# A layer-norm, attention and quantized-FFN kernel: statistics of the second half made ahead, block loads requested a step ahead, reloads in four parts

## What is computed

```python
xn = _layernorm(x, axis=-1)                       # x: 4 x 1024 x 1024, f32
s = _L0_attn_ref(xn)                              # softmax over the 4 batch rows, per position l
g = _silu(_L0_ffn_ref(xn, gate_codes, gate_scales, up_codes, up_scales, down_codes, down_scales))
x = x + s * g
# _L0_ffn_ref: NF4 codes (blocks of 64) are turned into Wg, Wu (2752 x 1024) and Wd (1024 x 2752), then
gate = jnp.einsum('bsh,ih->bsi', x, Wg)
up = jnp.einsum('bsh,ih->bsi', x, Wu)
inter = jax.nn.silu(gate) * up
return jnp.einsum('bsi,hi->bsh', inter, Wd)
```

## Time and profile before

| what | us |
|---|---|
| median of 3 runs | 2674.68 (2670.05 to 2675.88) |
| profiled execution | 2672.88, of it 2671.1 between first and last instruction |
| PE busy | 2445.3 (92%) |
| DVE busy | 1650.6 (62%) |
| ACT busy | 1010.7 (38%) |
| first product of step 5 to first product of step 45 | 242.58 to 1091.28 |

### The profile page before, as it was taken

The page is one execution under the profiler, slowest core; times in us unless marked ns, Lnnn a source line. Parts: engine busy times, 40 slices in busy tenths (PEclk is TensorE's granted clock), DMA queues, the critical chain, the costliest instruction groups (busy, mean ns, idle before and its releaser), DMA issues.

```text
span 2671.1 us, 30439 instructions
## 1 busy us (share of the span) xinstructions
PE 2445.3 (92%) x11214; PEld 1114.0 (42%) x11214; DVE 1650.6 (62%) x2721; ACT 1010.7 (38%) x1303; POOL 457.0 (17%) x318
## 2 busy tenths in 40 slices
PE   2459999898888897999999999999999999999999
PEld 1224444443333343444444444444444444444444
DVE  6767877876687774678788788655451341341341
ACT  5467666566666652444545542111001000000000
POOL 3441111112222211111111011112011011011011
PEclk9679999999999998999999999999999999999999
DMA  6354555655656547665655564324886776776864
GB/s 220 105 165 155 183 174 189 193 174 181 221 178 210 172 147 294 234 216 192 202 195 207 197 203 172 135 91 166 319 334 247 326 286 255 323 280 260 325 273 158
DMA packets 176016, 571.14 MB, mean 214 GB/s; under 512 B 23968, under 2 KB 49232, under 8 KB 158076
## 3 DMA queue, kind: packets, MB, share of 16 engines
q1 hardware_dynamic: 140876, 280.82, 30.7%
q10 hardware_dynamic: 34992, 288.37, 28.6%
HBM read 380.38 MB, written 188.75 MB: 213 GB/s over the span
## 4 chain that ended last, share of the span: by engine, by line
PE 66%; DVE 12%; issue 7%; DMA 6%; POOL 5%; ACT 3%; SPq 1%; DVEq 0%; POOLq 0%; ACTq 0%
PE ps L1554 37%; PE ps L1683 29%; DVE arena L1220 3%; DMA arena<-xnsc 3%; DMA isc<-arena 1%; POOL arena L707 1%; DVE arena L1164 1%; ACT arena L756 1%; DVE arena L1189 1%; DMA arena<-in_gu 1%; POOL arena L678 1%; DVE arena L1214 1%; POOL arena L704 1%; DVE st L1104 1%; ACT arena L890 1%
## 5 line engine op out<-in xcount | busy, mean ns | idle before, releaser
L1554 PE MATMUL ps<-arena 128*128 128x512 f16 x7200 | 1600.5, 385 | 118.6 <-ACT arena L931 45.3
L1554 PEld LDWEIGHTS ps<-arena 128*128 128x128 f16 x7200 | 710.5, 99 | 996.3 <-issue 62.5
L1683 PE MATMUL ps<-arena 128*128 128x512 f16 x3696 | 797.9, 379 | 0.0
L756 ACT ACTIVATE arena<-arena,bias_t 128x1024 f32<-128x1024 f32 (+1 forms) x520 | 574.3, 1141 | 41.9 <-DMA arena<-in_gu 27.9
L1683 PEld LDWEIGHTS ps<-arena 128*128 128x128 f16 x3696 | 361.6, 98 | 436.1
L1220 DVE TENSOR_TENSOR arena<-arena 128x512 f16<-128x512 f32 x364 | 310.8, 864 | 63.4 <-ACT arena L890 62.2
L697 POOL TENSOR_TENSOR arena<-arena 128x512 f32<-128x512 f32 x52 | 77.2, 1484 | 1066.3 <-DVE arena L1347 894.4
L1214 DVE CAST arena<-arena 128x512 f16<-128x512 f32 x308 | 172.0, 570 | 132.5 <-POOL arena L707 59.5
L721 POOL TENSOR_TENSOR arena<-arena 128x512 f32<-128x512 f32 x64 | 82.2, 1292 | 686.6 <-DMA arena<-in_xt 385.3
L931 ACT ACTIVATE arena<-ps,gate_back 128x512 f32<-128x512 f32 x84 | 57.4, 683 | 364.8 <-PE ps L1554 364.6
L1072 ACT ACTIVATE arena<-arena,e_d 128x512 f32<-128x512 f32 x48 | 34.6, 721 | 424.3 <-DVE arena L1483 219.4
(11 more groups left out here) (109 smaller groups left out, 1329.8 us busy)
## 6 DMA issues: line engine op xcount, KB each, us to landing
isc<-arena SPq DMA_DIRECT2D x308, 256.0 KB, 2.0
arena<-wdsc ACTq DMA_DIRECT2D x28, 2816.0 KB, 10.0
arena<-isc ACTq DMA_DIRECT2D x28, 2816.0 KB, 18.2
arena<-xnsc SPq DMA_DIRECT2D x48, 1024.0 KB, 10.7
wsc<-arena ACTq DMA_DIRECT2D x21, 1792.0 KB, 6.6
arena<-in_gu ACTq DMA_DIRECT2D x43, 512.0 KB, 4.1
wdsc<-arena SPq DMA_DIRECT2D x77, 256.0 KB, 2.1
arena<-in_x SPq DMA_DIRECT2D x32, 512.0 KB, 5.9
```

What stands on the lines that cost most here:

```text
L756: a_.activation(buf, src, ACT.Prelu, bias=bias_t[:, i:i + 1], scale=scale, alpha=alpha).then_inc(ramps, 1)
L1554: ins = t_.matmul(ps[:, bank, :], wreg[:, b, w, wa, k, :], xreg[:, j, o, k, xa, :], start=start and (k, wa, xa) == (0, 0, 0), stop=stop an ...
L1683: ins = t_.matmul(ps[:, bank, :], ring_w[b][:, k, wa, g, :], ring_i[b][:, k, xa, :], start=first and (k, wa, xa) == (0, 0, 0), stop=r not ...
```

## The change

Five edits.

1. The statistics of tiles 16 to 31 are no longer made in pairs beside their normalisation. The tiles are loaded once more and their statistics taken in steps 4 (six tiles, one in each slot), 6 and 7 (five each, slots 0 to 4). SP loads tile tt+2 when the statistics of tile tt are done, since there are two slots. All 16 are aggregated and all roots taken in slot 1 of step 8. Tiles are normalised from step 8 on, a pair every second step (`NORM_AT` 8 to 22), the first in slot 4, the second in slot 5.
2. The x jobs move from steps 22 to 35 to steps 26, 27, 30, 31, 34, 35, 38, 39. Their blocks are requested one step earlier on SP.
3. The x jobs of even steps (26, 30, 34, 38) have their casts on VectorE and their items in slots 0 to 2 (`SOON_CUT`); those of odd steps (`X_ACT`) keep the casts on ScalarE.
4. `reloads` takes a part, 0 to 3; the transfers of steps 41 to 45 are dealt out to the start of ScalarE's step, after its first ramps, after `sil_a`, and after its second ramps.
5. In step 44 the items of the down weights move from slot 1 to slot 5, and after a LAST step the two memsets come behind the product that TensorE waits for.

```diff
-NORM_AT = {6 + 2 * i: (16 + 2 * i, 17 + 2 * i) for i in range(8)}
-XJOB_AT = {s: (2 + i // 4, i % 4) for i, s in enumerate([s for s in SPARE if s >= 22][:8])}
+STAT_AT = {4: range(16, 22), 6: range(22, 27), 7: range(27, 32)}
+ROOTS_AT = 8
+NORM_AT = {8 + 2 * i: (16 + 2 * i, 17 + 2 * i) for i in range(8)}
+XJOB_AT = {s: (2 + i // 4, i % 4) for i, s in enumerate([s for s in SPARE if s >= 24][-8:])}
+X_ACT = [XJOB_AT[s] for s in XJOB_AT if PASS[s][1]]
...
+SOON_CUT = [0, 6, 10, 14, 14, 14, 14]
...
-                if tt == 16:
+                if tt >= 16:
+                    sp.wait_ge(stat, 32)
+                    if nat_use(tt):
+                        sp.wait_ge(xs_out[nat_slot(tt)], 16 * nat_use(tt))
...
+            def load_stat(tt):
+                h, n, q = tokens(tt)
+                if tt < 18:
                     sp.wait_ge(e_lo, 5 * 7)
+                else:
+                    sp.wait_ge(stat, 2 * (tt - 18) + 2)
+                sp.dma_start(nat[nat_slot(tt)], x[n, h * CH + q * P:h * CH + (q + 1) * P, :]).then_inc(nat_in[nat_slot(tt)], 16)
...
-                if s in XJOB_AT:
-                    load_blocks(("x",) + XJOB_AT[s])
+                if s + 1 in XJOB_AT and s not in XJOB_AT:
+                    load_blocks(("x",) + XJOB_AT[s + 1])
...
+                if s + 1 in XJOB_AT and s in XJOB_AT:
+                    load_blocks(("x",) + XJOB_AT[s + 1])
...
+                if s == 3:
+                    load_stat(16)
+                    load_stat(17)
+                for tt in STAT_AT.get(s, ()):
+                    if tt + 2 < 32:
+                        load_stat(tt + 2)
...
-                    if s == 41:
-                        act.wait_ge(prod, prod_at(40, "p5"))
-                        load_xb(0, 5)
-                        load_xb(0, 6)
-                        act.wait_ge(prod, prod_at(39, "p3"))
-                        load_w(0, 4, 7)
-                        load_w(0, 2, 4)
-                    elif s == 42:
-                        act.wait_ge(prod, prod_at(41, "r"))
-                        act.wait_ge(prod, prod_at(40, "p3"))
-                        for o in (0, 4, 2, 3):
-                            load_xb(0, o)
+                if (s, part) == (41, 0):
+                    act.wait_ge(prod, prod_at(40, "p5"))
+                    load_xb(0, 5)
+                elif (s, part) == (41, 1):
+                    load_xb(0, 6)
+                elif (s, part) == (41, 2):
+                    act.wait_ge(prod, prod_at(39, "p3"))
+                    load_w(0, 4, 7)
+                elif (s, part) == (41, 3):
+                    load_w(0, 2, 4)
+                elif (s, part) == (42, 0):
+                    act.wait_ge(prod, prod_at(41, "r"))
+                    act.wait_ge(prod, prod_at(40, "p3"))
+                    load_xb(0, 0)
...
+            def stats(tt):
+                dve.wait_ge(nat_in[nat_slot(tt)], 16 * nat_use(tt) + 16)
+                for k in (0, 1):
+                    v_.bn_stats(st2[:, tt - 16, 6 * k:6 * k + 6], nat[nat_slot(tt)][:, 512 * k:512 * k + 512]).then_inc(stat, 1)
...
-                if s in DOWN_AT and slot == (5 if jobs else 1):
+                if s in DOWN_AT and slot == (5 if jobs or s == NSTEP else 1):
                     d_items(*DOWN_AT[s])
...
-                if s in NORM_AT and slot == 3:
-                    lnorm(NORM_AT[s], 2)
+                for tt in list(STAT_AT.get(s, ()))[slot:slot + 1]:
+                    stats(tt)
+                if s == ROOTS_AT and slot == 1:
+                    all_roots()
+                if s in NORM_AT and slot >= 4:
+                    normal(NORM_AT[s][slot - 4])
```

More of the change, by code:

```diff
@@ L106 @@
 JOB = {c: i for i, c in enumerate(JOBS)}
-INNER = {c: i for i, c in enumerate(c for c in JOBS if c[0] == "i")}
+CAST_HERE = {c: i for i, c in enumerate(c for c in JOBS if c[0] == "i" or c[1:] not in X_ACT)}
 NEARLY = 8
@@ L851, in reloads @@
                     load_w_second(1)
-                    for o in (0, 4, 2, 3):
-                        load_xb(1, o)
-                elif s == NSTEP + 1:
+                    load_xb(1, 0)
+                elif (s, part) == (NSTEP, 1):
+                    load_xb(1, 4)
+                elif (s, part) == (NSTEP, 2):
+                    load_xb(1, 2)
+                elif (s, part) == (NSTEP, 3):
+                    load_xb(1, 3)
+                elif (s, part) == (NSTEP + 1, 0):
                     act.wait_ge(prod, prod_at(43, "p2"))
                     load_w(0, 1, 2)
+                elif (s, part) == (NSTEP + 1, 1):
                     load_xb(1, 1)
+                elif part or h == 0:
+                    return
                 elif s == NSTEP + 3:
@@ L1107, in lnorm, with roots @@
                     step(v_.bn_aggr(mv[:, i, :], st[:, i, :]), i == m - 1)
-                va, r, t = y[:, 0, 0:m], y[:, 1, 0:m], y[:, 2, 0:m]
-                step(v_.tensor_scalar(va, mv[:, 0:m, 1], EPS, 2.0 ** (-2 * XS), ALU.add, ALU.mult))
+                roots(mv[:, 0:m, 1], y[:, 0, 0:m], y[:, 1, 0:m], y[:, 2, 0:m], True)
+                dve.wait_ge(ln_out, tiles[0] // 8 + 1)
+                for i, tt in enumerate(tiles[:mine]):
+                    v_.tensor_scalar(nat[nat_slot(tt)], nat[nat_slot(tt)], mv[:, i, 0:1], y[:, 1, i:i + 1],
+                                     ALU.subtract, ALU.mult).then_inc(xn_done, 1)
+            def roots(var, va, r, t, shared):
+                step(v_.tensor_scalar(va, var, EPS, 2.0 ** (-2 * XS), ALU.add, ALU.mult))
                 step(v_.tensor_scalar(r.bitcast(I32), va.bitcast(I32), -0.5, float(0x5F375A86), ALU.mult, ALU.add))
@@ L1315, in background @@
                 for c in jobs:
-                    for i in range(JOB_CUT[slot], JOB_CUT[slot + 1]):
+                    at = SOON_CUT if c[0] == "x" and c[1:] not in X_ACT else JOB_CUT
+                    for i in range(at[slot], at[slot + 1]):
                         c_item(c, i)
```

87 lines of the change are left out of this document (56 added, 31 removed).

## The result

| | us |
|---|---|
| before, median of 4 runs | 2673.91 (2670.05 to 2675.88) |
| after, median of 4 runs | 2653.93 (2650.41 to 2658.59) |
| ratio | 0.9928, 95% interval 0.9907 to 0.9949 |
| predicted | 2617, range 2599 to 2636 |
| profiled execution | 2672.88 before, 2658.59 after; between first and last instruction 2671.1 and 2656.8 |

The kernel is 0.7% faster, some 20 us, where 57 were forecast. The sign was right, and the size lies outside the range. Ratios leave out one execution that was far slower at a lower granted clock (2712.66 us, experiment 8); the median and the span given there still count it.

A forecast was written before the change was run, and what follows sets the result against it. TensorE, busy 92%, was taken as the bound, losing 119.4 us to waits and slow clock. After: 18 + 10.3 + 31 + 5.3 = 64.6, so 54.8 won from 2672.9: 2618, stated as 2617 us, range 2599 to 2636.

The forecast's parts named there:

- The sum: Steps 5 to 45: TensorE's losses fall from 119.4 to 64.6 us, so 54.8 us are won.
- The 10.3 us of silA I leave: Steps 11, 15, 19, 23: waits for silA stay at 10.3 us, as loads keep their order beside the same steps.
- Statistics: Steps 4 to 8: statistics made ahead stand at loads and delay c21; 18 us lost, 10 more than before.
- p7(7), forecast at 2.3 us: Step 6's statistics make c21(5) late: a wait of 2.3 us, and 1.3 for the clock.
- Steps 13, 17, 21: Normalisation and c21 waits go once statistics leave steps 12, 16 and 20: 21.4 us won.
- x cycles: Four cycles from step 24, VectorE the bound, block landing 8.5 us: 31 us lost against 59.8 before.
- the wait of 7.29 us the largest: Steps 24 to 37: the wait in front of the cycle from 650.21 was called the largest, 7.29 us.
- The turn: Reloads dealt out and down-weight items moved to slot 5: 5.3 us lost against 20.0 before.
- I keep 2 us of the 12.85, bounds 0 and 8: Step 42: of TensorE's 12.85 us wait for c21(40) at p7(42), 2 us remain, between 0 and 8.
- bound by bytes, not by their order: Rival, chance 0.08: at the turn the 12.85 us come back nearly whole, 2628 us.
- only about 1 MB at a time now stands before a store: Turn: the same bytes are moved, but with only about 1 MB at a time before a store; part of the 5.3 us term.
- Casts beside GpSimd's sums: Even x jobs on VectorE: first two casts could take 1.84 us beside a sum; each step could cost a sum's length more.

The follow-up runs named there:

- experiment 8: Changed kernel with the turn's reloads of x in order of first use and spread over one step more: 2657.63 us, ratio 0.9947.
- experiment 2: Changed kernel with four ramps, not five, ahead of sil_a in even steps 4 to 38: 2640.83 us, ratio 0.9882.
- experiment 4: Changed kernel with the first pair of x blocks of each cycle requested behind the stage stores, not ahead: 2641.68 us, ratio 0.9886.
- experiment 6: Changed kernel with only a quarter of each x-operand load at the turn (256 KB in place of 1 MB): 2641.47 us in one run.
- experiment 1: Changed kernel with edit 1 undone, statistics back beside the normalisation in steps 6 to 20: 2654.07 us, ratio 0.9933.
- experiment 5: Changed kernel with the high parts of all eight x blocks cast on ScalarE, as before: 2651.19 us, ratio 0.9927.
- experiment 7: Kernel before with edits 4 and 5 alone: 2668.25 us beside 2669.78, ratio 0.9996.

## Why the prediction was wrong in size

**The sum.** 54.8 us were to be won from step 5 to step 45. By the same count 16.7 were (119.4 less 102.7), and the profiled execution is 14.3 us shorter. Of the 38 us between, 14 are at sil_a, 17 in steps 24 to 39 and 11 at the turn as far as step 45, less 2 that the statistics cost less than forecast. That is 2 us too many, since the places are waits and slow clock, while the total charges each step 18.29 us. That is from a step's first start to its last end; from start to start a step without a wait takes 18.13 us (experiment 2: 38.01 us for two with four half tiles). So the work is 723 us and not 729.7, and 125 us were lost before and 109 after; the difference stays. Three terms failed, by 11 to 17 us each in this execution. For each there is a run that takes its cause away and is 12 to 13 us faster than the changed kernel by the medians (experiments 2, 4 and 6, the last a single execution).

**"The 10.3 us of silA I leave": a step that failed (24 measured, 16 to 24 in five executions).** It argued that SP's and the code loads' order beside those steps stays the same. It does. But how long TensorE waits depends on its own position too: each pause of TensorE, 5 us in every fourth step, was also a head start for ScalarE and VectorE. With it gone, the ramps of steps 14 and 18 start at 9.4 to 10.3 us into TensorE's step in place of 6.7 to 8.4, and sil_a is as much later, with the slow clock on top. Experiments 1 and 2 show the coupling: undoing edit 1 brings sil_a's waits from step 5 to 24 down from 18.3 to 7.4 us, and moving one ramp takes those of steps 11 to 23 away. The term should have been worked out like the others: when does ScalarE reach its fifth ramp, if TensorE no longer waits?

**Statistics (18 forecast, 16 measured).** The size was near, and the mechanism right in the main: VectorE stands at loads of x, and TensorE for c21 at p7(5) and longest in step 9 (6.24 us, forecast 7.0, though at the normalised tile and not at c21). Two errors in it cancel. VectorE's waits for the tiles were 0.6 to 3.2 us each, not a whole landing, since its other work covered part of each round, and at p7(7), forecast at 2.3 us, TensorE didn't wait. But it waited 3.84 us at p7(6), with 2.7 of slow clock, which was put at nothing: the sixth tile of step 4 stands behind c21(3), VectorE waits 3.19 us for it, and so is late with c21(4).

**Steps 13, 17, 21 (0 forecast, 0 measured).** Right. Yet the gain of 21.4 us was not the kernel's: with the edit undone the median is the same (experiment 1), and step 24 starts at 637.1 us, in the midst of the 633.5 to 643.5 of the changed kernel's executions.

**x cycles (31 forecast, 48 measured): a cost put at nothing.** The blocks' landing was near (8.5 to 10.3 us for 8.5). The casts moved to VectorE bought nothing (experiment 5): a block cast there trades a wait for sil_a for one for c21. (The prediction also called the wait of 7.29 us the largest; the one at 739.40 has 7.65.) The step that failed is this: two loads of 512 KB requested ahead of seven stage stores on the same queue were taken as free for the stores. They cost VectorE 17.1 us of stage slots, and the kernel 12 us (experiment 4).

**The turn (5.3 forecast, 17.6 measured).** "I keep 2 us of the 12.85, bounds 0 and 8": 6.91 was left, within the bounds. Put at nothing were the slow clock behind it (2.9), the weight block's wait (3.1) and a c21 just behind step 45 (1.5). The order of the requests counted, for VectorE's slot waits fell from 20.0 to 11.4 us. But the rival "bound by bytes, not by their order", given 0.08, holds for the rest: requests dealt out leave 18 us of loss (experiment 7), and with a quarter of the bytes 5.7 are left (6). The step that failed is "only about 1 MB at a time now stands before a store". The loads of 1 MB were requested 6.0 and 11.5 us apart and took 10.9 us to land (median), with a weight store and weight loads between them, so that from 1000.3 to 1030.0 some transfer of ScalarE's queue was always under way. The Trainium skill (DMA: Bandwidth & Descriptors, "Queues, rings and completion order") says that each DMA engine changes between the queues that have work, packet by packet. The landing of 10.0 us for a store beside the loads and 5.4 beside quarter loads agrees with it: a store shares for as long as any load is under way. By that, the rival deserved a larger chance. And the load of weight block (0,0,1) in step 43 was overlooked: it now stands behind a load of 1 MB on its queue, 3.1 us.

**Casts beside GpSimd's sums.** The prediction weighed that an instruction on VectorE is slower while GpSimd makes a sum. In the x jobs moved to VectorE it didn't happen, since GpSimd's first sums are over by then: the first two casts at 779.38 took 0.75 us, against 1.84 in an inner job. It reached another place: a low part of a weight block at 770.72 took 1.76 us, while GpSimd's first sum of x ran, against 0.69 us for the one at 764.32. About 1 us a place; it decides nothing here.

## What to carry to other kernels

A wait on the engine that bounds is also slack for the others: before counting it as won, work out when each of them would be late if that engine came on at once. A term left "as it is" needs the same arithmetic as one that changes. And a load requested early is not free for the stores queued or under way beside it: what counts is bytes in the stretch and who holds a buffer until they have landed.

## What the runs showed of the hardware

- A store of 256 KB took 10.0 us to land beside loads of 1 MB on another queue and 5.4 beside loads of 256 KB (median of those issued from 1000 to 1024 us), and 2.0 us at 993.8, with nothing beside it. The mean DMA share over 985 to 1030 us was 0.77 and hid where the stores were held. In pieces of 5 us (the share is the last number but one) it is 0.49 ahead of the loads and 1.04 beside them:

```profile
995.00:1000.00 5.00, 5.00 (x24) 2.24 (x23) 3.54 (x7) 2.38 (x3) 1.28 (x1) 1.00 0.49 185
1010.00:1015.00 5.00, 5.00 (x25) 2.29 (x24) 1.63 (x3) 1.84 (x3) 0.80 (x1) 1.00 1.04 397
```

- Waits of 3.06 to 5.14 us in every fourth step brought 7.3 us of slow clock with them (24 products in 6.8 to 8.1 us for 5.35), 0.43 us for each us of waiting. But the price of one wait can't be told from its length. In experiment 5 the products behind a wait of 3.71 us took 5.35 us, as without one, and smaller waits were not always cheaper: in experiment 2 the two steps around waits of 1.58 and 0.39 us took 40.35 us, those around one of 2.17 us 42.05, where two such steps without a wait took 38.01.
